# A two-attention block with experts: q and k projected by tokens, their parts turned to rows by 16-bit transposes

## What is computed

```python
# first half, per item: layer norm, shift and factor, attention with a learned position bias
q, k, v = [shape(h @ W.T) for W in (Wq, Wk, Wv)]           # 16 heads of 8
attn = softmax(q @ k.T * 8**-0.5 + position_bias)
x1 = x + gate_a * ((attn @ v) @ Wo.T)
# second half: layer norm, shift and factor give hb; then a decoder layer on hb
r = rmsnorm(hb, g1)
q, k, v = r @ wq, r @ wk, r @ wv
q = q * cos + rotate_half(q) * sin                         # k the same way
attn = softmax(causal(q @ k.T * 8**-0.5))
h2 = hb + (attn @ v) @ wo
r2 = rmsnorm(h2, g2)
# 8 experts, the best 2 for each token, weights by softmax: (silu(r2@wg) * (r2@wu)) @ wd
```

## Time and profile before

| what | us |
|---|---|
| median of three runs | 1074.74 |
| lowest and highest run | 1070.42, 1076.9 |
| the profiled execution, its own time | 1070.41 |
| its span, first to last instruction | 1068.3 |
| TensorE busy | 907.6 |
| VectorE busy | 698.0 |
| ScalarE busy | 529.0 |
| GpSimd busy | 227.1 |

### The profile page before, as it was taken

How to read it: one execution, slowest core, us unless ns; L and a number is a source line. 1 busy time by engine, 2 the same in 40 slices (tenths; PEclk the granted TensorE clock), 3 DMA queues, 4 the chain that set the end, 5 groups by cost and what they waited for, 6 DMA issues and landing times.

```text
span 1068.3 us, 36323 instructions
## 1 busy us (share of the span) xinstructions
PE 907.6 (85%) x15358; PEld 560.1 (52%) x15358; DVE 698.0 (65%) x1534; ACT 529.0 (50%) x908; POOL 227.1 (21%) x274
## 2 busy tenths in 40 slices
PE   6776878988899998898899699989899777887893
PEld 3343434545455554455444345555456466776792
...
PEclk9889999699999999999998699999898999999896
...
GB/s 202 165 312 182 313 22 8 2 7 3 27 17 13 27 13 12 7 23 17 17 13 15 27 13 13 3 17 18 12 25 24 27 55 61 61 57 180 121 62 118
DMA packets 50045, 61.74 MB, mean 58 GB/s; under 512 B 5600, under 2 KB 36064, under 8 KB 49504
## 3 DMA queue, kind: packets, MB, share of 16 engines
...
## 4 chain that ended last, share of the span: by engine, by line
PE 46%; DVE 24%; issue 13%; ACT 8%; POOL 4%; another core or an unknown queue 3%; DMA 2%; POOLq 0%; SPq 0%; DVEq 0%; ACTq 0%
DVE row_max L1188 14%; PE ps L838 8%; PE ps L689 5%; PE ps L722 5%; PE ps L734 4%; PE ps L923 3%; PE ps L670 3%; POOL eo_rows L1477 3%; PE ps L700 2%; PE ps L664 2%; ACT stage L963 2%; ACT k_head L963 2%; PE ps L728 1%; PE ps L915 1%
## 5 line engine op out<-in xcount | busy, mean ns | idle before, releaser
L1188 DVE TENSOR_REDUCE row_max<-ps 128x4 f32<-128x1024 f32 (+1 forms) x256 | 266.1, 1079 | 57.0 <-PE ps L700 30.6
L1025 ACT ACTIVATE probs<-ps 128x1024 f32<-128x1024 f32 x128 | 130.0, 1027 | 104.5 <-PE ps L722 89.1
L1025 ACT ACTIVATE stage<-ps 128x1024 f32<-128x1024 f32 x96 | 98.0, 1024 | 88.8 <-PE ps L728 79.9
L689 PE MATMUL ps<-bias_t,ch 64*32 64x512 f16 x2048 | 112.2, 408 | 26.9 <-DVE row_max L1188 18.1
L1477 POOL DMA_INDIRECT eo_rows<-eo_t,to_t x92 | 88.8, 965 | 117.7 <-ACT eo_t L1075 98.6
L1432 POOL TENSOR_TENSOR rstd_n<-var_n,cf 128x2 f32<-128x2 f32 x48 | 34.4, 717 | 370.8 <-DVE var_n L1125 370.6
L915 PE MATMUL ps<-xT_t,wgu_hi 128*128 128x256 f16 x276 | 77.2, 280 | 21.3 <-DVE hid L1360 12.5
L1355 DVE SCALAR_TENSOR_TENSOR gate_s<-gate_t,ps 128x256 f32<-128x256 f32 x138 | 57.4, 416 | 48.1 <-ACT gate_t L1069 41.8
...
L838 PE MATMUL ps<-probs,v_pad 128*32 128x256 f32 x1024 | 84.9, 399 | 1.9 <-issue 1.2
L1069 ACT ACTIVATE gate_t<-ps 128x256 f32<-128x256 f32 x138 | 52.5, 383 | 63.3 <-PE ps L917 42.3
L689 PEld LDWEIGHTS ps<-bias_t,ch 64*32 64x32 f16 x2048 | 30.0, 91 | 101.5 <-DVE row_max L1188 44.5
...
## 6 DMA issues: line engine op xcount, KB each, us to landing
...
```

The lines of the kernel that those rows point to most:

```text
L689: eng.matmul(ps[HR * c:HR * (c + 1), lo + r, :].rearrange("p (j s) -> p j s", j=2), csth("flip")[half, :], bias_t[half, way, 2 * g:2 * g + ...
L1025: eng.activation(probs[a][:, 2 * (k % 2):2 * (k % 2) + 2, :], ps[:, lo:lo + 2, :], ACT.Exp).then_inc(z["exp"], 1)
L1188: ins = eng.tensor_reduce(row_max[a][:, qt, 4 * g:4 * g + 4].rearrange("p (r j) -> p r j", r=2), of_heads, AX.X, ALU.max)
```

## The change

q and k of a token are now projected together, with 128 tokens as the stationary operand and the two weights beside each other (256 columns) as the moving one: two products in place of two for `f1` and of four for `f2`. Tokens are on the partitions afterwards. The swapped weights `q2r` and `k2r` are gone: `sin` reads the other half of each head by its address, in four instructions of 128 columns. The factor of the rms norm `r1` is not spread over the channels any more (`spread.r1`, `n.r1` and `rT` are gone); it enters as one scalar per token in `cos`, in `sin` and when the values are written to `v_pad`, and `g1` is multiplied into the weights once. So `qk` of `f2` waits for `n2` alone, and `var.r1` becomes a stream of its own on TensorE (`pe_root`).

`qk_tok` holds, for each token, q or k and head, 32 float16 places with the parts in the order of the rows. `hi` writes one of them, a new ScalarE step `again` of two instructions copies it to the second place, and `lo` becomes two instructions of 256 columns. `pe_spread` has two steps, `k` and `q`, each of eight float16 transposes of 128 by 128 into one bank read as float16. ScalarE takes them out in instructions of 1024 columns: two for k, one for q. In the second attention the values are written in four instructions in place of two. GpSimd clears `qk_tok` once for each attention, ahead of the clearing of `v_pad`. The tables of `cos` and `sin`, the 0/1 matrices and the swapped weights leave the constants, which makes the loads at the start smaller. The durations in `Plan` change with the steps.

```diff
-WA = ("q1", "k1", "v1", "o1a", "o1b", "q2", "k2", "q2r", "k2r", "v2", "o2a", "o2b")
+WA = ("q1", "k1", "v1", "o1a", "o1b", "q2", "k2", "v2", "o2a", "o2b")
...
-        for n in ("k0", "k1", "q0", "q1"):
-            self.op((job, i, n), "pe", 0.44, [last] + ([("c%d" % a, i - 2, "end")] if i > 1 else []), SHARED)
-            self.op((job, i, "row." + n), "act", 1.1 if n[0] == "k" else 0.60, [(job, i, n)], (), "mine")
-        self.op((job, i, "end"), None, 0.0, [(job, i, "row." + n) for n in ("k0", "k1", "q0", "q1")])
+        again = self.op((job, i, "again"), "act", 0.7, [(job, i, "hi")])
+        for n, us in (("k", 2.1), ("q", 1.05)):
+            self.op((job, i, n), "pe", 0.5, [last, again] + ([("c%d" % a, i - 2, "end")] if i > 1 else []), SHARED)
+            self.op((job, i, "row." + n), "act", us, [(job, i, n)], (), "mine")
+        self.op((job, i, "end"), None, 0.0, [(job, i, "row." + n) for n in ("k", "q")])
...
-        last = self.chain("f2", i, last, ("sq.r1", "act", 0.42))
-        last = self.norm("f2", i, "r1", last, False)
-        self.chain("f2", i, last, ("qk", "pe", 0.9, SHARED), ("cos", "dve", 0.69, (), "mine"))
-        last = self.chain("f2", i, last, ("qkr", "pe", 0.9, SHARED), ("sin", "dve", 0.69, (), "mine"))
-        last = self.op(("f2", i, "sum"), "dve", 0.69, [last, ("f2", i, "cos")])
-        last = self.chain("f2", i, last, ("hi", "act", 0.62), ("lo", "dve", 0.69))
+        self.op(("f2", i, "qk"), "pe", 0.9, [last], SHARED)
+        self.chain("f2", i, last, ("sq.r1", "act", 0.42), ("var.r1", "pe", 0.33, SHARED), ("v.r1", "dve", 0.16, (), ("f2", i, "var.r1")))
+        root = self.op(("f2", i, "root.r1"), "pool", 0.72, [("f2", i, "v.r1")] + ([("c2", i - 2, "vz")] if i > 1 else []))
+        self.op(("f2", i, "cos"), "dve", 0.75, [("f2", i, "qk"), root])
+        last = self.op(("f2", i, "sin"), "dve", 0.9, [("f2", i, "cos")], (), ("f2", i, "qk"))
+        last = self.chain("f2", i, last, ("sum", "dve", 0.69), ("hi", "act", 0.62), ("lo", "dve", 0.75))
...
+            qk_tok[a] = sb("qk_tok%d" % a, [P, KT, 2, H, HR], F16)
...
+        def by_head(x):
+
+            return x.rearrange("p (t w h d) -> p t w h d", t=KT, w=2, d=HD)
+
+        def turn(name, t, d, n):
+
+            table = cst(name)[:, t * HD + d:t * HD + d + n]
+            return table.unsqueeze(1).to_broadcast([P, 2 * H, n])
...
-            for e in range(2):
-                dst = bank[:, e * S:(e + 1) * S]
-                cols = slice((g + e) * P, (g + e + 1) * P)
-                eng.matmul(dst, csth(n + "_hi")[:, cols], qk_hi[a][:, col:col + S], start=True, stop=False)
-                ins = eng.matmul(dst, csth(n + "_lo")[:, cols], qk_lo[a][:, col:col + S], start=False, stop=True)
...
-        def pe_project(eng, bank, names, src):
-            for k, n in enumerate(names):
-                ins = eng.matmul(bank[:, k * S:(k + 1) * S], W[n], src, start=True, stop=True)
+        def pe_project(eng, bank, a, src):
+
+            first = WA.index("q%d" % a)
+            for t in range(KT):
+                ins = eng.matmul(bank[:, t * S:(t + 1) * S], src[:, t * P:(t + 1) * P], wa[:, first:first + 2, :],
+                                 start=True, stop=True)
             return ins
 
         def pe_spread(eng, a, job, i, at):
 
             z = att[a]
-            for n, e in (("k", 0), ("k", 1), ("q", 0), ("q", 1)):
-                yield at(n + str(e))
-                bank = free_bank(eng, job, i, n + str(e))
-                if n == "k" and e == 0:
+            for w, n in ((1, "k"), (0, "q")):
+                yield at(n)
+                flat = free_bank(eng, job, i, n).bitcast(F16)
+                if n == "k":
+                    eng.wait_ge(z["again"], i + 1)
                     eng.wait_ge(z["lo"], i + 1)
-                pe_rows(eng, a, n, 2 * e, bank).then_inc(z[n + "spread"], 1)
+                for g in range(NG):
+                    for t in range(KT):
+                        heads = qk_tok[a][:, t, w, 4 * g:4 * g + 4, :].rearrange("p h m -> p (h m)")
+                        ins = eng.transpose(flat[:, g * S + t * P:g * S + (t + 1) * P], heads, ident_h)
+                ins.then_inc(z[n + "spread"], 1)
...
-            yield from pe_norm(eng, "r1", "f2", i, at)
             yield at("qk")
             bank = free_bank(eng, "f2", i, "qk")
             if i == 0:
-                eng.wait_ge(su["casts"], 2)
-            eng.wait_ge(norm["r1"]["n"], i + 1)
-            pe_project(eng, bank, ("q2", "k2"), rT[:, i % 2, :]).then_inc(z["qk"], 1)
-            yield at("qkr")
-            bank = free_bank(eng, "f2", i, "qkr")
-            pe_project(eng, bank, ("q2r", "k2r"), rT[:, i % 2, :]).then_inc(rot_done["qkr"], 1)
+                eng.wait_ge(su["casts"], 3)
+            eng.wait_ge(norm["n2"]["h"], i + 1)
+            pe_project(eng, bank, 2, hbT[:, i % 2, :]).then_inc(z["qk"], 1)
...
+            eng.activation(qk_tok[a][:, :, :, :, 0:HD].rearrange("p t w h d -> p (t w h) d"),
+                           src.rearrange("p (n d) -> p n d", d=HD), ACT.Copy).then_inc(att[a]["hi"], 1)
+            yield again
+            eng.wait_ge(att[a]["hi"], i + 1)
+            for w in range(2):
+                ins = eng.activation(qk_tok[a][:, :, w, :, (1 + w) * HD:(2 + w) * HD], qk_tok[a][:, :, w, :, 0:HD], ACT.Copy)
+            ins.then_inc(att[a]["again"], 1)
...
-                yield at("row.k%d" % e)
-                eng.wait_ge(z["kspread"], 2 * i + e + 1)
-                if i > 1:
-                    eng.wait_ge(z["wscore"], n_u[a] * (i - 1))
-                for j in range(HJ):
-                    ins = eng.activation(k_head[a][:, b, 2 * e:2 * e + 2, j, :], halves(held(job, i, "k%d" % e)), ACT.Identity,
-                                         bias=cst("kones")[:, j:j + 1], scale=cst("kmask")[:, j:j + 1])
-                ins.then_inc(z["krow"], 1)
-            for e in range(2):
-                yield at("row.q%d" % e)
-                eng.wait_ge(z["qspread"], 2 * i + e + 1)
-                if i > 1:
-                    eng.wait_ge(z["wscore"], n_u[a] * (i - 1))
-                eng.activation(q_rows[a][:, b, 2 * e:2 * e + 2, :], halves(held(job, i, "q%d" % e)),
-                               ACT.Copy).then_inc(z["qrow"], 1)
+            yield at("row.k")
+            eng.wait_ge(z["kspread"], i + 1)
+            if i > 1:
+                eng.wait_ge(z["wscore"], n_u[a] * (i - 1))
+            for j in range(HJ):
+                ins = eng.activation(k_head[a][:, b, :, j, :], held(job, i, "k").bitcast(F16).rearrange("p (g s) -> p g s", g=NG),
+                                     ACT.Identity, bias=cst("kones")[:, j:j + 1], scale=cst("kmask")[:, j:j + 1])
+            ins.then_inc(z["krow"], 1)
+            yield at("row.q")
+            eng.wait_ge(z["qspread"], i + 1)
+            if i > 1:
+                eng.wait_ge(z["wscore"], n_u[a] * (i - 1))
+            eng.activation(q_rows[a][:, b, :, :], held(job, i, "q").bitcast(F16).rearrange("p (g s) -> p g s", g=NG),
+                           ACT.Copy).then_inc(z["qrow"], 1)
...
+                for n, gain in (("q2", gain_q[:, :]), ("k2", gains[:, 0:1]), ("v2", gains[:, 0:1])):
...
+                if a == 1:
+                    ins = eng.activation(dst[:, :, e, :, 8 * e:8 * e + 8], v_ps[:, :, e, :, :], ACT.Copy)
+                else:
+                    for t in range(KT):
+                        ins = eng.activation(dst[:, 2 * t:2 * t + 2, e, :, 8 * e:8 * e + 8], v_ps[:, 2 * t:2 * t + 2, e, :, :],
+                                             ACT.Copy, scale=rstd_r1[:, i % 2, t:t + 1])
...
+        def dve_lo(eng, a, src, i, at):
+            z, tok = att[a], qk_tok[a]
+            yield at("lo")
+            eng.wait_ge(z["hi"], i + 1)
+            for w, lo in ((0, 2 * HD), (1, HD)):
+                ins = eng.tensor_tensor(tok[:, :, w, :, lo:lo + HD], by_head(src)[:, :, w, :, :], tok[:, :, w, :, 0:HD], ALU.subtract)
+            ins.then_inc(z["lo"], 1)
...
-            yield from dve_norm(eng, "r1", "f2", RMS_EPS, hbT[:, i % 2, :], gains[:, 0:1], rT[:, i % 2, :], None, i, at)
+            yield from dve_var(eng, "r1", "f2", RMS_EPS, i, at)
             yield at("cos")
             eng.wait_ge(z["qk"], i + 1)
-            eng.tensor_tensor(halves(rot[:, 0, :]), halves(held("f2", i, "qk")), twice("cos"), ALU.mult).then_inc(rot_done["cos"], 1)
+            eng.wait_ge(norm["r1"]["root"], i + 1)
+            qk, cos, sin = [x.rearrange("p (t n d) -> p t n d", t=KT, d=HD) for x in (held("f2", i, "qk"), rot[:, 0, :], rot[:, 1, :])]
+            for t in range(KT):
+                eng.scalar_tensor_tensor(out=cos[:, t, :, :], in0=qk[:, t, :, :], scalar=rstd_r1[:, i % 2, t:t + 1],
+                                         in1=turn("cos", t, 0, HD), op0=ALU.mult, op1=ALU.mult).then_inc(rot_done["cos"], 1)
             yield at("sin")
-            eng.wait_ge(rot_done["qkr"], i + 1)
```

(15 more changed lines are left out.)

108 lines of the change are left out of this document (56 added, 52 removed).

## The result

| | before | after |
|---|---|---|
| median of four runs each, us | 1072.97 | 1058.41 |
| lowest to highest | 1070.42 to 1076.9 | 1052.17 to 1062.33 |
| profiled execution, us | 1070.41 | 1060.48 |

A few executions that took over 1.5% more than the fastest of their kernel are left out of all ratios and mean clocks. The ratio is 0.9849, with a 95% interval of 0.9807 to 0.9891: 1.5% less time. Two more series of the same kernel gave 0.9855 (0.9805 to 0.9905) and 0.9795 (0.9767 to 0.9824). The mean of the three, 0.983, is 18 us. The forecast was 34.6 us, so half of it came, though the time lies within the range of 1012 to 1066.

What follows compares the result with a forecast made beforehand. Attentions were taken as bound by TensorE for some 59% of the time and VectorE about a quarter. TensorE -38.0, VectorE +3.0 and ScalarE +0.4 gave -34.6 us: 1035.8 profiled, median 1040, range 1012 to 1066.

Steps and rivals of the forecast that it cites:

- The transposes: Row steps of each attention: eight float16 transposes take 0.55 us to the next step, priced from `max_rows`.
- The third rival: Row transposes don't gain: their term shrinks from 27.5 to 6.7 us, giving 1053 us; chance 0.08.
- TensorE's work: 59.9 us less at full clock: rows 27.5, their pauses 5.8, `f2` projections 16.8, spread of `r1` 9.8.
- the two terms for pauses between steps: TensorE pauses of 0.09 us each saved: up to 5.8 us at the row steps, and one per item in `f2`.
- VectorE: Rotation and `lo` in `f1` and `f2`: 0.78 us more per item, 12.5 us in all, counted as +3.0.
- ScalarE: Copies, row exits and value writes in the attentions: 0.28 us more per item, 4.5 in all, counted as +0.4.
- the step -38.0: TensorE's 64.4 us saved in the attentions, counted with 59%, become 38.0 us less time.
- the chain's share of 59%: Share of the chain that ended last, PE 46% plus issue 13%, by which TensorE's saved time was counted.
- The rival in which it falls more often: TensorE idles more beside row maxima, so half-clock stretches grow; 1099 us at twice as many; chance 0.07.
- the first and largest term: Rows in 32 attentions: 16 transposes take 1.10 us in place of 1.96 for 16 products, 27.5 us gained.
- everything converts: TensorE sets the pace nearly everywhere, so all 64.4 us less 3.4 come back: 1014 us; chance 0.15.
- VectorE's turns decide: Score steps alternating with row maxima set the pace, TensorE's front work was filler: 1060 to 1075 us; chance 0.13.

Runs made afterwards that it cites:

- no_lo_before: Kernel before the change, with the products of the low parts left out of the rows, order unchanged: +0.35% (+3.8 us), ratio 1.0035.
- nudge_after: Changed kernel with one constant of the plan moved, the assumed delay from TensorE to another engine 0.27 in place of 0.25 us: ratio 0.9824 to the kernel before.
- the last two kernels of the table: Kernel before without the low-part row products (1.0035), and also without one of two products in the turned projection and the `r1` spread (0.9973).
- the pair with both fillings: Changed kernel and kernel before, each with score steps doubled where the plan idles TensorE, and idle products ahead of two waits: 0.9801 and 0.9972.
- sin_plain: Changed kernel with `sin` in one instruction of 256 columns per 128 tokens, without the exchange of halves: ratio 0.9819 to the kernel before.
- plan_true: Changed kernel with the plan's durations set to those that follow from its profile: ratio 0.9875 to the kernel before.

## Why the prediction was right or wrong

**The transposes** were right: 0.53 us for eight where 0.55 stood. The third rival falls with them.

**TensorE's work** was forecast to shrink by 59.9 us, and shrank by 48 to 51 by the table. Without the two terms for pauses between steps (5.8 and 16 x 0.09 = 1.4) the forecast would be 52.7. Those pauses were idle time and not work; that term was put in the wrong place.

**VectorE** was oversized in what it costs the engine: 12.5 us forecast, 4.2 measured in busy time. Count times mean would give 13, so the durations were right, and the overlap of instructions in a row makes the difference. **ScalarE** was undersized, 7.8 in place of 4.5. Both are small.

**What failed is the step -38.0**, in which the 64.4 us count with the chain's share of 59% at an unchanged clock of 0.93. Both of its halves failed.

*The clock.* The sum divided by 0.93 and so kept the clock as it was. The rival in which it falls more often had the mechanism, the place and a price per microsecond of "up to half", but a chance of 0.07, and was thought of only as a case that turns the sign. It came true in part, as a term within the forecast. The argument against it, that 300 to 400 us would stay full, was wrong: that stretch went from 1.00 to 0.91, 0.95 and 0.97 in three profiles. On two chips the change has 35 and 24 us more at half clock; at 0.29 to 0.38 us each (the correlation within one kernel), that is 7 to 13 us of the 17 that are missing.

*The share of 59%.* It took all of TensorE's work as alike. Of its two parts, the 13% of "issue" was read as the small pauses between TensorE's steps. The chain of the kernel before, in order of time, has 74 us of issue up to 845 us, and the largest piece stands behind a step of GpSimd, in a stretch in which TensorE was busy all the time (20.70 of 20.70 us):

```profile
307.41 20.74 issue
```

Pieces under 0.3 us make up 18 us of the 74. And the first and largest term, the row products, gained nothing when it was taken away alone (*no_lo_before*, +3.8 us). The attentions, which should have ended 35 us earlier, ended 3 to 7 us earlier with two more tiles beside them, and 13 us earlier in *nudge_after* with as many as before.

That the time fell within the range of 1012 to 1066 says little for the sum: the range was wide enough for half the gain. Of the signs of being wrong one came, more idle time behind the row maxima (40.7 to 46.5 us), and one just not, a clock under 0.9 before the experts (0.91).

How much each term weighs I took from the first 18 kernels of the table by least squares, with the ratio times 1070.4 as the time:

| time = 496 + a x work + b x half-clock time | a | b | spread of the rest |
|---|---|---|---|
| from the ratios | 0.61 (+-0.06) | 0.35 (+-0.05) | 3.4 us |
| from the profiled spans (constant 429) | 0.68 | 0.48 | 3.4 us |

In these kernels a microsecond of TensorE's work goes with about 0.6. The change has 50 us less work, -30.5, and on the two chips with clocks on record 35 and 24 us more at half clock, +12 and +8; together -18 and -22, where -15.5 and -22 was measured there. As a sum this closes. But the last two kernels of the table are left out, and they are the ones that only take work away. With them the fit gives 0.42 (+-0.12) and 0.21 (+-0.09) with a spread of 8 us. It describes a family in which most kernels add work to the new order.

Two things keep it from being a proof of the cause. In the pair with both fillings the half-clock times are equal and the work is 42 us apart, so that the fit gives 26 us, and 18 came; with intervals of 5 us this is a weak sign. The strong one is that the two kernels with less work in the old order gained nearly nothing on their chip, though their clock was read. So it is shown that half-clock time rose with the change, that it depends on where TensorE's work stands relative to the row maxima, and that filling those places lowers it. That the clock alone ate the missing 17 us is not shown, and by the price within one kernel it ate 7 to 13 of them. What stays open is whether the change's gain comes from less work, or from shorter paths with two steps for four and a rotation that waits for less. The changed projection alone in the old order, with profiles of before on the same chip, would tell.

The other rivals: *everything converts* (1014) is excluded by the result, *VectorE's turns decide* (1060 to 1075) had the right neighbourhood of times. Its first half, that TensorE's front work was filler and taking it away frees nothing, fits *no_lo_before*. Its second, late `cos`, `sin` and `lo`, isn't seen in *sin_plain* and *plan_true*, though TensorE does wait longer for VectorE. Its upper end is mis-summed: with 38 us for short runs the case gives 1060 + 38 = 1098, and not 1075.
